# Feed-forward of each chunk in two halves of tokens on one PSUM bank, and a fourth bank for the ring of row maxima

## The reference

```python
x = x + xcond0(layernorm(x), ctx, tau, fside)   # 16 heads of 16 features over 1601 context rows: softmax(scale*(q@k*tau + fside)) @ v @ Wo
x = x + ffn0(layernorm(x))                      # router over 8 experts, top 1: y = (x @ expert_w[e] + expert_b[e]) * prob
x = x + xcond1(ctx, layernorm(x), len, p_t)     # window of keys around p_t: softmax, gauss, tanh([context, x] @ W_c)
x = x + ffn1(layernorm(x))                      # gelu, top 8 of 64 slots, slots updated by a GRU and attention, read back by the tokens
```

## Time and profile before

| | |
|---|---|
| median of 3 runs | 1086.86 us (1086.31 to 1095.68) |
| profiled execution | 1086.41 us, span 1084.4 us |
| mean granted TensorE clock | 0.968 |
| start and chunk 0 | until 250 us |
| chunk 1, chunk 2, chunk 3 | 250 to 493, to 735, to 967 us |
| end | 967 to 1084 us |

### The profile page before, as it was taken

The page is one execution under the profiler, slowest core; times in us unless marked ns, Lnnn a source line. Parts: engine busy times, 40 slices in busy tenths (PEclk is TensorE's granted clock), DMA queues, the critical chain, the costliest instruction groups (busy, mean ns, idle before and its releaser), DMA issues.

```text
span 1084.4 us, 13614 instructions
## 1 busy us (share of the span) xinstructions
PE 978.2 (90%) x4794; PEld 390.6 (36%) x4794; DVE 745.5 (69%) x1704; ACT 571.3 (53%) x1063; POOL 63.8 (6%) x91
## 2 busy tenths in 40 slices
PE   6799999999889999989889989989989999889986
PEld 3453323323333334423323333423333333334643
DVE  4688888887677777776677777776767764235634
ACT  2456766666454456665445546665445547740330
POOL 3441000000000000000000000000000000100000
PEclk9899999999899989999899989999899989999999
DMA  7936500001000000001000000001000000140022
GB/s 187 200 73 111 121 1 15 16 1 35 1 16 1 16 1 14 3 1 55 1 16 1 15 1 13 3 1 54 1 15 1 0 2 1 40 125 2 1 97 78
DMA packets 33931, 36.19 MB, mean 33 GB/s; under 512 B 6670, under 2 KB 30523, under 8 KB 33603
## 3 DMA queue, kind: packets, MB, share of 16 engines
q1 hardware_dynamic: 32542, 34.17, 12.5%
q10 hardware_dynamic: 1242, 0.90, 0.6%
q0 software_dynamic: 80, 0.26, 0.1%
HBM read 21.55 MB, written 7.35 MB: 27 GB/s over the span
## 4 chain that ended last, share of the span: by engine, by line
issue 51%; PE 30%; DVE 9%; DMA 2%; ACT 2%; POOL 2%; DVEq 2%; SPq 1%; POOLq 0%; ACTq 0%
PE ps_m L1064 7%; PE ps_o L1148 7%; PE ps_e L1350 5%; DVE mx L1651 4%; PE ps_e L1022 2%; DMA xres<-in_x 1%; PE ps_m L1350 1%; SPq L545 1%; PE ps_m L1168 1%; PE ps_m L1298 1%; POOL rstd L684 1%; POOL xres L735 1%; PE ps_m L1301 1%; DVE xn L1643 1%; DMA x<-xres 1%
## 5 line engine op out<-in xcount | busy, mean ns | idle before, releaser
L1651 DVE TENSOR_REDUCE mx<-ps_m 128x1 f32<-128x401 f32 x1024 | 538.3, 568 | 198.0 <-PE ps_m L1064 190.6
L848 ACT ACTIVATE probs<-ps_e 128x512 f32<-128x512 f32 (+1 forms) x763 | 437.1, 598 | 342.2 <-PE ps_e L1350 340.5
L1064 PE MATMUL ps_m<-k_stack,q_stack 99*128 99x401 bf16 x1024 | 319.4, 343 | 36.6 <-DVE mx L1651 34.9
L1350 PE MATMUL ps_e<-q_stack,k_stack 101*128 101x512 bf16 (+1 forms) x763 | 299.5, 394 | 10.9 <-ACT probs L848 8.7
L1148 PE MATMUL ps_o<-probs,v_heads 128*32 128x512 f32 (+1 forms) x1664 | 228.9, 623 | 0.0
L1350 PEld LDWEIGHTS ps_e<-q_stack,k_stack 101*128 101x128 bf16 (+1 forms) x763 | 75.9, 100 | 261.8 <-ACT probs L848 167.7
L1064 PEld LDWEIGHTS ps_m<-k_stack,q_stack 99*128 99x128 bf16 x1024 | 102.0, 100 | 183.8 <-DVE mx L1651 131.0
L1252 PE MATMUL ps_m<-expert_w,xnT 128*128 128x512 f32 x192 | 99.4, 598 | 15.2 <-DVE xb L1788 15.2
L1148 PEld LDWEIGHTS ps_o<-probs,v_heads 128*32 128x32 f32 (+1 forms) x1664 | 33.1, 109 | 60.7 <-issue 49.4
L848 ACT ACTIVATE probs<-ps_m 128x512 f32<-128x512 f32 (+1 forms) x69 | 41.6, 603 | 15.2 <-PE ps_m L1350 15.1
L1788 DVE SCALAR_TENSOR_TENSOR xb<-ps_m,hot,xb 128x256 f32<-128x256 f32 x84 | 40.6, 484 | 7.9
(11 more groups left out here) (333 smaller groups left out, 720.0 us busy)
## 6 DMA issues: line engine op xcount, KB each, us to landing
q_stack<-q_parts SPq DMA_DIRECT2D x78, 64.0 KB, 2.6
expert_w<-in_expert_wT SPq DMA_DIRECT2D x2, 1024.0 KB, 12.9
xres<-in_x SPq DMA_DIRECT2D x4, 512.0 KB, 3.8
x<-xres SPq DMA_DIRECT2D x4, 512.0 KB, 3.2
probs<-x SPq DMA_DIRECT2D x1, 2048.0 KB, 8.5
k_stack<-alphaT SPq DMA_DIRECT2D x10, 200.1 KB, 7.6
probs<-in_ctxT SPq DMA_DIRECT2D x3, 512.0 KB, 7.5
q_parts<-probs SPq DMA_DIRECT2D x4, 384.0 KB, 3.0
```

The source lines that it names most:

```text
L848: act.activation(probs[0:n, k % 2, h, :], score_bank(c, k, h)[0:n, :], ACT.Exp).then_inc(s["exp_done"], 1)
L1064: pe.matmul(ps_m[:, (UNITS * n1 + u) % RING, 0:SPLIT], qst[0:MAX_ROW, g, h, P * t:P * t + P], kst[0:MAX_ROW, HG * g + h, QUARTER_START[q]: ...
L1350: pe.matmul(score_bank(c, k, h)[0:n, :], kst[0:ROWS, HG * g + h, P * st:P * st + n], qst[0:ROWS, g, h, :], start=True, stop=True).then_inc ...
L1651: dve.tensor_reduce(mx[:, q, col:col + 1], ps_m[:, (UNITS * n1 + u) % RING, 0:SPLIT], AX.X, ALU.max)\
```

## The change

The feed-forward of chunks 0 to 2, which before went in steps of a whole chunk, now goes in two chains, one for each half of 256 tokens (two tiles), with the same functions as the end of the kernel; a third chain (`choice`) has h, logits, slots and alphaT for the whole chunk. All of these jobs, o and m use a single bank, `ps_m[:, 3]`, each after the one before. `ps_m[:, 4]` joins the ring: from unit WIDE = 336 on, near the start of chunk 1, four banks take turns, and TensorE may be four units ahead. `HALF_STEPS` replaces `JOBS`; its entries are name, predecessor, lag and hold, and `places()` interleaves the chains, so that a job starts where the hold of the one before has ended. An expert job is still 128 tokens by two experts, but written as two times 256 columns, in two neighbouring quarters. GpSimd makes the reciprocal root of each half by itself (six steps a chunk instead of three), and semaphores are kept for each half. The end of the kernel keeps its four banks and its order; its expert products too are written by 256 columns.

```diff
+WIDE = (UNITS * (NG + 1) + LEAD + 11) // 12 * 12
...
-JOBS = [("ota", None, 10, 3), ("otb", "ota", 2, 3), ("y0", "otb", 3, 3), ("y1", "y0", 2, 3), ("t1a", "y1", 11, 3),
-        ("t1b", "t1a", 2, 3), ("router", "t1b", 3, 2), ("e0", "router", 5, 6)]
-JOBS += [(f"e{i}", f"e{i - 1}", 4, 6) for i in range(1, 4)] + [("gateT", "e3", 3, 3), ("e4", "gateT", 1, 6)]
-JOBS += [(f"e{i}", f"e{i - 1}", 4, 6) for i in range(5, NE)]
-JOBS += [("gb0", f"e{NE - 1}", 4, 4), ("gb1", "gb0", 2, 4), ("t2a", "gb1", 11, 3), ("t2b", "t2a", 2, 3),
-         ("score0", "t2b", 3, 3), ("score1", "score0", 2, 3), ("aTa", "score1", 13, 3), ("aTb", "aTa", 2, 3),
-         ("z0", "aTb", 3, 9), ("z1", "z0", 8, 9), ("t3a", "z1", 20, 3), ("t3b", "t3a", 2, 3), ("h", "t3b", 3, 5),
-         ("logits", "h", 6, 2), ("slots", "logits", 14, 6), ("alphaT", "slots", 4, 3)]
+HALF_STEPS = [("ot", None, 10, 3), ("y", "ot", 3, 3), ("t1", "y", 8, 3), ("router", "t1", 3, 2), ("e0", "router", 7, 4),
+              ("e1", "e0", 4, 4), ("gateT", "e1", 4, 2)]
+HALF_STEPS += [(f"e{i}", f"e{i - 1}", 4, 4) for i in range(2, NE // 2)]
+HALF_STEPS += [("gb", f"e{NE // 2 - 1}", 4, 4), ("t2", "gb", 8, 3), ("score", "t2", 3, 3), ("aT", "score", 9, 3), ("z", "aT", 3, 5), ("t3", "z", 11, 3)]
+LAST_STEPS = [("h", "t3", 3, 4), ("logits", "h", 4, 2), ("slots", "logits", 13, 5), ("alphaT", "slots", 5, 3)]
 
...
-    ring, at = [(0, 0), (0, 0)], {}
-    for name, after, lag, hold in JOBS:
-        q = at[after] + lag if after else lag
+    ring, at = [(0, 0)], {}
+
+    def earliest(name, after, lag, h):
+        if name == "ot" and h:
+            return at.get(("t1", 0), NEVER) + 4
+        if name == "e0" and h:
+            return max(at.get((f"e{NE // 2 - 1}", 0), NEVER) + 4, at.get((after, h), NEVER) + lag)
+        if name == "h":
+            return max(at.get((after, half), NEVER) for half in range(2)) + lag
+        if after is None:
+            return lag
+        return at.get(after if h is None else (after, h), NEVER) + lag
+
+    todo = [(0, list(HALF_STEPS)), (1, list(HALF_STEPS)), (None, list(LAST_STEPS))]
+    while any(steps for _, steps in todo):
+        h, steps = min(((h, steps) for h, steps in todo if steps), key=lambda x: earliest(*x[1][0][:3], x[0]))
+        name, after, lag, hold = steps.pop(0)
+        q = max(earliest(name, after, lag, h), ring[-1][0])
         while True:
             while fixed and fixed[0][0] < q:
                 ring.append(fixed.pop(0))
-            q = max(q, ring[-2][1])
-            if not fixed or fixed[0][0] >= q and ring[-1][1] <= fixed[0][0]:
+            q = max(q, ring[-1][1])
+            if not fixed or q + hold <= fixed[0][0]:
                 break
             q = max(q, fixed[0][0] + 1)
-        at[name] = q
+        at[name if h is None else (name, h)] = q
         ring.append((q, q + hold))
     return at
...
+        def max_bank(n):
+            return ps_m[:, n % RING if n < WIDE else (0, 1, 2, RING + 1)[n % (RING + 1)], :]
...
-                need(pe, s["max_taken"], UNITS * n1 + u + 1 - RING)
-                pe.matmul(ps_m[:, (UNITS * n1 + u) % RING, 0:SPLIT], qst[0:MAX_ROW, g, h, P * t:P * t + P],
+                n = UNITS * n1 + u
+                if n == WIDE + RING:
+                    pe.wait_ge(s["exp_done"], HG * SLOTS)
+                need(pe, s["max_taken"], n + 1 - (RING if n < WIDE + RING else RING + 1))
+                pe.matmul(max_bank(n)[:, 0:SPLIT], qst[0:MAX_ROW, g, h, P * t:P * t + P],
...
+            def expert_half(i, c, h):
+
+                half_free(pe, f"e{i}", c, h)
+                tok, j = HC * h + P * (i // 4), i % 4
+                for e in range(2):
+                    for k in range(KT):
+                        if e and not k:
+                            yield AT[f"e{i}", h] + 1
+                        mm = pe.matmul(half_bank(f"e{i}", c, h)[:, D * e:D * e + D], xnT[:, k, tok:tok + P],
+                                       expert_w[:, k, CT * j + D * e:CT * j + D * e + D], start=(k == 0), stop=(k == KT - 1))
+                fills_half(mm, f"e{i}", c, h)
...
+            def take_expert(i, c, h):
+                t, j = HT * h + i // 4, i % 4
+                for e in (2 * j, 2 * j + 1):
+                    if e % 2:
+                        yield AT[f"e{i}", h] + 3
+                    dve.drain()
+                    if e % 2 == 0:
+                        wait_half_filled(dve, f"e{i}", c, h)
+                    last = dve.scalar_tensor_tensor(out=xb[:, t, :], in0=half_bank(f"e{i}", c, h)[:, D * (e % 2):D * (e % 2) + D],
+                                                    scalar=hot8[:, t, e:e + 1], in1=(xb if e else xa)[:, t, :],
+                                                    op0=ALU.mult, op1=ALU.add)
+                takes_half(last, f"e{i}", c, h)
...
+                sum_half(xa[:, tiles(h), :], xres[:, tiles(h), :], "y", c, h)
+                yield AT["y", h] + 3
+                yield from stats_half(xa, h, AT["y", h] + 4)
+                yield AT["t1", h] - 1
+                normal_half(xa, 0, c, h)
+                yield AT["router", h] + 1
+                gate_logits(c, h)
+                yield AT["router", h] + 2
+                gate_top(h)
+                yield AT["router", h] + 3
+                gate_first(h)
+                yield AT["router", h] + 6
+                gate_weight(c, h)
+                for i in range(NE // 2):
+                    yield AT[f"e{i}", h] + 2
+                    yield from take_expert(i, c, h)
+                yield AT["gb", h] + 3
+                dve.drain()
+                sum_half(xb[:, tiles(h), :], xb[:, tiles(h), :], "gb", c, h)
+                yield AT["gb", h] + 4
+                yield from stats_half(xb, h, AT["gb", h] + 5)
+                yield AT["t2", h] - 1
+                normal_half(xb, 1, c, h)
+                yield AT["score", h] + 2
+                window_scores(c, h)
+                yield AT["score", h] + 3
+                window_max(h)
+                yield AT["score", h] + 7
+                window_weights(c, h)
+                yield AT["z", h] + 5
+                third_sum(c, h)
+                yield AT["z", h] + 6
+                yield from stats_half(xres, h, AT["z", h] + 7)
+                yield AT["t3", h] - 1
+                normal_half(xres, 2, c, h)
```

More of the change, by code:

```diff
@@ L180, in job_numbers, with go_on, at_once @@
                 order.append(("o", NG * c + O_AT.index(q) - 1))
-        if c == 0:
-            first = len(order)
-        else:
+        if c:
             order += [(name, c - 1) for name in AT if AT[name] >= HG * SLOTS]
     order.append(("o", NG * NC - 1))
-    numbers = {job: (0, i) for i, job in enumerate(order[:first])}
-    numbers.update({job: (1 - i % 2, i // 2 + (first if i % 2 else 0)) for i, job in enumerate(order[first:])})
-    return numbers
+    return {job: i for i, job in enumerate(order)}
 def begin(steps):
     return [steps, next(steps)]
-def go_on(work, quarter):
-    while work and work[1] <= quarter:
-        work[1] = next(work[0], NEVER)
+def go_on(works, quarter):
+    for work in works:
+        while work[1] <= quarter:
+            work[1] = next(work[0], NEVER)
+def at_once(steps):
+    for _ in steps:
+        pass
 JOB = job_numbers()
@@ L211 @@
 HC = CT // 2
-NORMS = NC + 3 * (NC - 1)
+NORM_ORDER = sorted((AT[name, h] + lag, i, h) for i, (name, lag) in enumerate((("y", 4), ("gb", 5), ("z", 7))) for h in range(2))
 def out_bank(c, i):
@@ L914, in chunk @@
             def chunk(c):
-                work = begin(behind(c - 1)) if c else None
+                work = [begin(steps) for steps in (behind(c - 1, 0), behind(c - 1, 1), choice(c - 1))] if c else []
                 for k in range(SLOTS):
@@ L1219, in behind @@
+            def behind(c, h):
+                yield AT["ot", h]
+                if c == 0 and h == 0:
                     pe.wait_ge(s["ld_fill"], N_FILL)
@@ L1822, in behind @@
[L1822 to L1830 removed]
+                last.then_inc(a_half[h], 1)
```

948 lines of the change are left out of this document (379 added, 569 removed).

## The result

The changed kernel takes 1187.9 us (median of 4 runs, 1185.8 to 1190.3), the kernel before 1087.1 in the same measurement: ratio 1.091 (95% interval 1.085 to 1.097), 101 us slower. The forecast was 1130, the range ended at 1165.

A forecast was written before the change was run, and what follows sets the result against it. TensorE, busy 90% of the span, sets the pace. New handovers of 24 us less a gain of 10 give 14 us in chunks 1 and 2 each, plus 15 in chunk 3: +43 us, forecast 1130 us, range 1096 to 1165.

The forecast's parts named there:

- The sum of the handovers: Single feed-forward bank, chunks 1 to 3: new waits cost 24 us each in chunks 1 and 2, 15 in chunk 3.
- the gain: Ring's fourth bank and VectorE's work spread by halves, chunks 1 and 2: 10 us saved a chunk, none in chunk 3.
- the clock: TensorE's granted clock in chunks 1 to 3, 0.96 to 0.97 before: the sum has no term for a change.
- Products by 256 columns: Expert products written in two parts: nothing, 0.3 us a chunk at most.
- The unit price of a close handover: TensorE waiting for VectorE to empty the single bank in the quarter just before: a stall of 0.94 us.
- nearly nothing with the product with the values between: Single-bank handovers with the values' product (a good 1 us) between emptying and next job: almost free.
- down to a third: Sign that the forecast is right: TensorE's waits for the ring's reductions fall to a third.
- Rival (c): TensorE's clock falls more often in chunks 1 to 3: +6 us a chunk, +18 us, 1148 us; chance 0.12.
- Rival (d): Single-bank handovers cost what the worst cost in the old kernel, 1.6 us: 1162 us; chance 0.06.
- (a): Handovers under 0.45 us, fourth ring bank gives back 15 to 20 us a chunk: 1063 us; chance 0.12.
- (b): Handover cost and ring gain cancel: 1087 ± 10 us; chance 0.10.
- (e): The ring is not four deep; the code shows it is, with one wait of at most 1 us; no chance given.

The follow-up runs named there:

- before256: The kernel before, with each expert product of chunks 0 to 2 written as two times 256 columns: 1089.7 us, ratio 1.002.
- ring3: The changed kernel with its single job bank but the ring three deep throughout, one bank unused: 1179.9 us, and 1184.0 when measured again.
- twobanks: The changed kernel with its halves and order, but feed-forward jobs on two banks in turn and the ring three deep: 1083.4 us, ratio 0.996.
- exp_alt: The changed kernel, ring of three; only expert halves take the other of two banks than the job before them: 1146.6 us.
- oth_alt: The changed kernel, ring of three; only jobs other than expert halves take the other of two banks than the job before: 1123.7 us.
- early_ring3: The changed kernel, ring of three, with VectorE's normalisations and second multiply-add of each expert half one quarter earlier: 1131.4 us.
- fill4: The changed kernel, ring of three, with four unread f32 products of 512 columns before each expert half's wait: 1309.5 us.
- fill_bf16: The changed kernel, ring of three, with four unread bf16 products before each expert half's wait: 1196.1 us, ratio 1.098.

## Why the prediction was wrong

The direction was right, and so was the main mechanism, handovers on the single bank. The size was not: 43 us forecast, 101 measured. Three terms of the sum failed. The sum of the handovers was 25 us too small, the gain some 14 too large, and the clock, some 20 us, stood in it at nothing. By its own steps:

- **Products by 256 columns, nothing.** Right (`before256`, 2 us).
- **The unit price of a close handover, 0.94 us.** Right where it was derived: 5.54 us a slot against 4.57 for the same slots with two banks. That it costs nearly nothing with the product with the values between was not always so (0.44 us of empty array at slot 9).
- **The sum of the handovers, 24 + 24 + 15 = 63 us.** This is the largest miss: 97 us measured, 88 of them at full clock. `ring3` against `twobanks`, from the two traces with the clock's part taken out at 0.36, is 31, 30 and 26 us for chunk 1, chunk 2 and from chunk 3 to the end. The price held, the sum was short everywhere, most in chunk 3, where I had set the handovers behind the last maxima low. Which of the counted handovers were underpriced is not shown one by one; the expert halves cost 37 us at full clock (`exp_alt`), the others 46 (`oth_alt`).
- **The gain, 10 us in chunks 1 and 2.** Here the reasoning failed. I took the gain out of the waits of the earlier trace rows (9.8 to 28.3 us). These did go, as forecast ("down to a third"), and gave next to nothing: the halves alone took them from 28.3 to 11.7 us in chunk 2, which lasted as long as before (`twobanks`). The spread of VectorE's work is worth 4 us in the whole run, 6 at full clock, and the fourth bank nothing: `ring3` should have been up to 20 us slower and is 6 to 8 faster, and equal at full clock. Waits at the ring were taken for time that can be had back. What a unit of lead is worth depends on the handovers, too (41 us with two banks, 6 with one).
- **The clock unchanged.** Wrong. Rival (c) named it, with two thirds more spells and +18 us, at a chance of 0.12. Measured are 123 to 127 us at 1.2 GHz after 69 to 74, and about 20 us. Its two errors nearly cancelled: it took half of the slowed time as lost, where 0.36 was measured, and in the profiled executions the time at 1.2 GHz in chunks 1 to 3 doubled, from 48 to 95 us. The page TensorE: Matmul & The Clock Gate of the Trainium skill ("A second HAM failure mode: psum-queue depth-cycling") had the direction. This case's traces agree with it in so far as the same instructions have 97 to 113 us at 1.2 GHz with one bank and 75 with two; but the regular stalls in front of the expert halves, which (c) had in mind, are not what brings them (`exp_alt`).

Together: 88 for the handovers, 20 for the clock, less 6 for the halves and 1 for the fourth bank, is 101, as measured. The parts are estimates at 0.36 us, and they were fitted to the same runs. Each miss pointed the same way, so the range did not hold it. Rival (d), dearer handovers, had the wrong price: the steady ones cost 0.97, not 1.6. Rivals (a) and (b) rested on the ring and fall with it. (e), that the ring is not four deep, is excluded by the code.

Not settled: why the clock is lower with the fourth bank and with the handovers of the jobs beside the expert halves, and what a fourth bank would be worth beside two job banks, for which the kernel has no bank left. The better kernel is `twobanks`: the halves with the old two banks, 0.4% faster than the kernel before.

## What to carry to other kernels

The total of the waits at a ring in the old profile is no estimate of what a deeper ring brings. In this kernel they are largely where VectorE's pace shows, and they move: 17 us of them went from chunk 2 without making it shorter. Price a single-buffer handover by the distance, in the written order, between the emptying step and the next filling one, and move the emptying step first: one quarter was worth 48 of 97 us here (`early_ring3` against `ring3`). Then add up every handover: the unit price was right, and the sum still a quarter to a third short. Where two kernels differ by less than 1%, compare their granted clocks before looking for a cause, and compare over all runs, since a single profiled execution can be the odd one. And where a forecast contains new stalls of TensorE, put its clock into the sum, at the cost that equal work at two clocks shows in the trace.

## What the runs showed of the hardware

- A us at 1.2 GHz cost this kernel 0.36 us, and not half of itself (34.84, 33.57 and 32.32 us for the same slots at 0.90, 0.95 and 1.00; 0.35 over 138 runs). TensorE's busy time rose more than the time did (30.15 against 27.09 us), so part of the slowed work lay in what had been waits.
- An f32 product of 512 columns holds TensorE 0.86 us (two recorded instructions, 0.43 apart), a bf16 one some 0.22 (`fill4`, `fill_bf16`).
- Steady slots repeat to 0.01 us from chunk to chunk once the clock is the same (slots 15 to 17 of the changed kernel: 16.63, 16.63 and 16.62 us), so small differences between kernels can be read from a few slots of one profile.
- The same instructions ran with 75 us at 1.2 GHz (`twobanks`), 97 and 113 (`ring3`) and 123 and 127 (changed kernel). The handovers of the jobs beside the expert halves carry the difference between the first two (`oth_alt` 71, `exp_alt` 109).
